# FFN weights compared in the opening, and the first tile's first FFN layer computed among the last tile's steps

## The reference

```python
xz = einsum('bld,ed->ble', x, in_proj_w)           # 256 -> 2 x 512, x and z
xc = silu(depthwise_conv4(x) + conv_b)             # u
dt_lo, B, C = split(einsum(u, x_proj_w), 64, 16, 16)
delta = softplus(einsum(dt_lo, dt_proj_w) + dt_proj_b)
h_t = exp(delta_t * A) * h_{t-1} + (delta_t * u_t) * B_t;  y_t = h_t . C_t   # 512 x 16 states
x1 = layernorm(x + einsum((y + u * D) * silu(z), out_proj_w))
h = silu((x1 @ w1) * s1) * ((x1 @ w2) * s2)        # 256 -> 1024
h = gelu((h @ h1) * sh1);  h = gelu((h @ h2) * sh2)   # 1024 -> 1024, twice
out = layernorm(x1 + (h @ w3) * s3)                # 1024 -> 256
```

## Time and profile before

| | us |
|---|---|
| median of 3 runs | 3138.71 (3132.48 to 3142.14) |
| profiled execution | 3133.98, span 3131.2 |
| PE, DVE, ACT, POOL busy | 2717.2, 2348.0, 2005.7, 1757.6 |
| first scan starts | 78.65 |
| last scan ends | 1963 |
| first matmul of the second stage | 2042.71 |

### The profile page before, as it was taken

The page is one execution under the profiler, slowest core; times in us unless marked ns, Lnnn a source line. Parts: engine busy times, 40 slices in busy tenths (PEclk is TensorE's granted clock), DMA queues, the critical chain, the costliest instruction groups (busy, mean ns, idle before and its releaser), DMA issues. The chain is left out here.

```text
span 3131.2 us, 39976 instructions
## 1 busy us (share of the span) xinstructions
PE 2717.2 (87%) x10900; PEld 1618.7 (52%) x10900; DVE 2348.0 (75%) x2845; ACT 2005.7 (64%) x3326; POOL 1757.6 (56%) x902
## 2 busy tenths in 40 slices
PE   5787887888887888888888885599999999999997
PEld 2243343333343343343333332478888888888886
DVE  2999999999999999999999999535444444444442
ACT  3767777767777767777777776545555545556542
POOL 0899899999899899899999899300000000000000
PEclk8788988988988889889889887799999999999999
DMA  5365466565465466465475465632222222222210
GB/s 136 92 189 160 121 190 160 126 182 150 121 193 162 124 180 162 115 194 150 130 191 144 133 188 166 247 107 81 86 75 67 94 67 80 88 72 74 87 41 14
DMA packets 236287, 402.54 MB, mean 129 GB/s; under 512 B 22977, under 2 KB 62145, under 8 KB 236097
## 3 DMA queue, kind: packets, MB, share of 16 engines
q1 hardware_dynamic: 174336, 293.48, 34.8%
q10 hardware_dynamic: 61760, 106.98, 10.6%
HBM read 276.12 MB, written 124.26 MB: 128 GB/s over the span
## 5 line engine op out<-in xcount | busy, mean ns | idle before, releaser
L1181 DVE TENSOR_TENSOR_SCAN h<-bank,state,db 128x512 f32<-128x512 f32 x1024 | 1252.9, 1266 | 61.5 <-ACT bank L863 34.4
L1044 POOL TENSOR_TENSOR hc<-h,c_rows 128x1024 f32<-128x1024 f32 x512 | 1200.7, 2375 | 28.1 <-PE bank L634 18.0
L863 ACT ACTIVATE bank<-d_bc,a_neg 128x512 f32<-128x512 f32 x1024 | 691.4, 685 | 345.8 <-DVE h L1181 230.5
L1523 ACT ACTIVATE s_h<-s_bank,sc 128x512 f32<-128x512 f32 x256 | 175.9, 687 | 494.0 <-PE s_bank L1462 493.7
L1462 PE MATMUL s_bank<-s_mid,h_r 128*128 128x512 f32 x2048 | 467.0, 389 | 0.0
L703 PE MATMUL bank<-x_t,w 128*128 128x512 f32 x1024 | 386.0, 506 | 75.1 <-ACT ab L933 35.9
L1165 DVE TENSOR_TENSOR db<-bank,du_bc 128x2048 f32<-128x2048 f32 x192 | 435.0, 2266 | 15.5 <-DMA du_bc<-du_rows 15.5
L1462 PEld LDWEIGHTS s_bank<-s_mid,h_r 128*128 128x128 f32 x2048 | 384.4, 188 | 80.1
L1055 POOL TENSOR_TENSOR db<-du_bc,b_row 128x2048 f32<-128x2048 f32 x64 | 291.0, 4547 | 104.3 <-DVE h L1181 98.6
L634 PE MATMUL bank<-hc,fold_w 128*32 128x512 f32 x2048 | 334.5, 732 | 7.2 <-DVE u L1205 4.4
L613 PE MATMUL bank<-bc,w_spread 64*128 64x512 f32 x272 | 154.4, 575 | 210.2 <-DVE db L1165 205.9
(11 more groups left out here) (140 smaller groups left out, 3584.1 us busy)
## 6 DMA issues: line engine op xcount, KB each, us to landing
ab<-ab ACTq DMA_DIRECT2D x264, 256.0 KB, 4.2
du_bc<-du_rows SPq DMA_DIRECT2D x256, 256.0 KB, 4.9
d_bc<-d_rows SPq DMA_DIRECT2D x256, 256.0 KB, 8.1
s_abr<-ab SPq DMA_DIRECT2D x120, 512.0 KB, 3.8
w<-w ACTq DMA_DIRECT2D x128, 256.0 KB, 3.6
d_rows<-sp_r SPq DMA_DIRECT2D x64, 256.0 KB, 2.0
du_rows<-sp_w SPq DMA_DIRECT2D x64, 256.0 KB, 2.0
x<-res SPq DMA_DIRECT2D x17, 512.0 KB, 9.3
```

The source lines that it names most:

```text
L863: act.activation(decays[DECAY_BANK[g]][:], d_bc[c % 2][:, j, :], ACT.Exp, scale=a_neg[:, g:g + 1]).then_inc(decay, 1)
L1044: pool.tensor_tensor(hc[:, k % HCSTEPS, at:at + HG], h[:, H_SLOT[k], at:at + HG], c_rows[:, q, :].unsqueeze(1).broadcast_to([P, HG, NT]), ...
L1181: dve.tensor_tensor_scan(h[:, H_SLOT[k], j, :], decays[DECAY_BANK[g]][:], db[:, k % DBSTEPS, j, :], state[:, g:g + 1], ALU.mult, ALU.add). ...
L1523: act.activation(hring[c % RING][:], p_h[m % HBANKS][:], ACT.Gelu, scale=sc[:, 2 + layer, m:m + 1]).then_inc(gelu, 1)
```

## The change

- Opening: SP loads all 18 pieces of h1, h2 and w3 behind w1 and w2 (`open_raw`, in the places of d_bc, du_bc, db, h, hc), POOL casts each into one of two buffers (`open_piece`), DVE compares (`check`): 14 pieces and the pieces of w1 before BEFORE's slots, four at slot 28. SP's first `copies` wait for 8 comparisons. The second rounding of w1/w2 pieces by ACT moves from slot 8 to 30, its comparison to slot 32.
- Last tile: ACT rounds h1's eight pieces at slots 8, 12, ..., 36; SP loads the first three ahead of `copies(t, 3)`, ACT's own queue the other five, a slot after a rounding. `first_abr` lies elsewhere. At slot 51 TensorE computes the first output of the first tile's h1 layer. ACT loads the table of Ln and Exp at slot 48.
- After it, the seven other outputs of that layer stand among norm, transposes and gate products (`closing` of pe and act); their gelu and high part on ACT, their low part on DVE behind the flag. h2's and w3's ten pieces are loaded by SP through three places instead of four and rounded by POOL, not compared; then the gate weights 2 to 7 are loaded in the places of the raw pieces (they were all eight loaded before). PAST's products use 4 banks instead of 8 and the copies a ring of 3 instead of 7. The end of these stores is waited for by SP in the second stage.
- Second stage: the first tile begins with `hidden(first, 1)`; the second tile's gate is made within that layer (`gate_steps`). First and second tile are unrolled, the loop begins at the third.

```diff
-W12_SLOTS = (2, 8)
+W12_SLOTS = (2, 30)
+CHECKS_FIRST, CHECK_SLOT, CHECK_W2_SLOT = 14, 28, 32
+ROUND_SLOTS = (8, 12, 16, 20, 24, 28, 32, 36)
+RAW_PLACES = 3
+GATE_SLOT, FIRST_SLOT = 42, 51
+FIRST_BANKS = (5, 6, 7, 3)
-PAST_RING = 7
-PAST_BANKS = (0, 3, 4, 5, 6, 7, 2, 1)
+PAST_BANKS = (0, 4, 2, 1)
 # sync, opening
+            for j in range(PIECES):
+                if open_bytes[j] == sb.first_byte["db"]:
+                    sp.wait_ge(consts, 1)
+                load_piece(sp, open_raw[j][:], j).then_inc(open_in[j], 16)
+            sp.wait_ge(checked, 8)
             copies(OPENING, 0)
 # sync, last tile and after
+                if t is LAST_ROW[-1]:
+                    closing_loads(t)
                 copies(t, 3)
...
             def closing(t):
                 for m in range(KH):
+                    if m == 2:
+                        sp.wait_ge(decay, t.count(NG, 3 * GC + DECAY0))
...
+                    elif m == 6:
+                        sp.wait_ge(h1_round, H1_PIECES)
                     sp.dma_start(first_abr[m][:], ...)
+                sp.wait_ge(first_lo, KH)
+                for j in range(RAW_PLACES + EARLY_POOL_PIECES):
+                    load_pool(j)
+                store_x1(PAST)
+                for j in range(RAW_PLACES + EARLY_POOL_PIECES, H2_PIECES + W3_PIECES):
+                    load_pool(j)
+                sp.wait_ge(pool_round, H2_PIECES + W3_PIECES)
+                for m in range(2, KH):
+                    sp.dma_start(past_w12[m][:].bitcast(F32), w12[m]).then_inc(past_w12_in, 16)
 # tensor
+            def first_layer(m):
+                if m >= len(FIRST_BANKS):
+                    pe.wait_ge(mid_gelu, m - len(FIRST_BANKS) + 1)
+                for k in range(KH):
+                    if m == 0:
+                        pe.wait_ge(first_lo, k + 1)
+                    for j in range(2):
+                        last = pe.matmul(bank[FIRST_BANKS[m % len(FIRST_BANKS)]][:], ...)
+                last.then_inc(mid_mm, 1)
+
+            def closing():
+                for m in (1, 2, 3):
+                    first_layer(m)
+                for k in range(KM):
+                    transposed(PAST, k, 0)
...
+                pe.matmul(p_y[:, 0:2 * KM + PIECES], ones[:], losses[:], start=True, stop=True).then_inc(counted, 1)
+                first_layer(4)
+                for k in range(KM):
+                    transposed(PAST, k, 2)
+                first_layer(5)
+                for e in range(AB):
+                    if e in (4, 8):
+                        first_layer(5 + e // 4)
+                    ffn_product(PAST, e)
 # scalar
+            def first_layer(m):
+                act.wait_ge(mid_mm, m + 1)
+                if m >= len(hring):
+                    act.wait_ge(mid_lo, m - len(hring) + 1)
+                act.activation(hring[m % len(hring)][:], ..., ACT.Gelu, ...).then_inc(mid_gelu, 1)
+                act.wait_ge(mid_gelu, m + 1)
+                act.activation(mid[0][:, m, :], hring[m % len(hring)][:], ACT.Copy).then_inc(mid_hi, 1)
+
+            def closing():
...
+                first_layer(5)
+                for e in range(AB):
+                    if e in (4, 8):
+                        first_layer(5 + e // 4)
+                    copy_product(PAST, e)
+                    store(PAST, e)
 # gpsimd
+            def open_piece(j):
+                pool.wait_ge(open_in[j], 16)
+                if j >= 2:
+                    pool.wait_ge(checked, j - 1)
+                pool.tensor_copy(open_r[j % 2][:], open_raw[j][:]).then_inc(open_round, 1)
+
+            for j in range(CHECKS_FIRST + 2):
+                open_piece(j)
             tile(BEFORE)
 # second stage
+        if t is not first:
+            return [(layer, m - 1)] if m else []
+        return [[], [(0, 0)], [(0, 1), (0, 2)], [(0, 3), (0, 4)], [(1, 0)], [(1, 1), (1, 2)], [(1, 3), (1, 4)], []][m]
...
+        for store_done, count in kept.stores:
+            sp.wait_ge(store_done, count)
...
+            pe.sem_inc(h_mm, KH)
+            hidden(first, 1)
+            output(first)
+            tile(second)
```

More of the change, by code:

```diff
@@ L366, in product_before @@
                     return before
+        kept.stores += [(ab_out[k], PAST.count(ab_uses(k), ab_uses(k) + ABOUT0)) for k in range(ABRING)]
         block = ctx.enter_context(nc.Block())
@@ L748, in _ @@
                 tile(t)
[L749 to L757, removed]
+            closing()
         @block.scalar
@@ L1100, in tile @@
                     n = OFF + i
+                    if t is BEFORE and i == CHECK_SLOT:
+                        for j in range(CHECKS_FIRST + 2, PIECES):
+                            open_piece(j)
                     if n % JC == 0:
@@ L1274, in tile @@
                         norm(t, i)
+                    if t is BEFORE and i == CHECK_SLOT:
+                        for j in range(CHECKS_FIRST, PIECES):
+                            check(j)
+                    if t is BEFORE and i == CHECK_W2_SLOT:
+                        for piece in range(KM, 2 * KM):
+                            check_w12(piece)
                     now, g = at_group(t, n)
@@ L1295, in tile @@
                         closing(t, i)
-            for piece in range(2 * KM):
-                check_w12(piece)
+            for j in range(CHECKS_FIRST):
+                if j == CHECKS_FIRST // 2:
+                    for piece in range(KM):
+                        check_w12(piece)
+                check(j)
             tile(BEFORE)
@@ L1379, in split_stage @@
     first = PairTile(0, 0)
+    second = first.following()
     last_pair = [PairTile(STEPS - 1, tt) for tt in range(2)]
@@ L1436, in body @@
             load(first)
-            load_half(first.following(), 0)
-            with sp.Fori(0, STEPS - 1) as b:
+            load_half(second, 0)
+            tile(first)
+            tile(second)
+            with sp.Fori(1, STEPS - 1) as b:
                 for tt in range(2):
@@ L1526, in hidden @@
                     act.activation(dst[:, m, :], hring[c % RING][:], ACT.Copy).then_inc(hi, 1)
-                    if m and exists(t.following()):
+                    if exists(t.following()):
                         if layer == 0 and m == 1:
                             act.wait_ge(o_mm, t.count(SUB, OUT0))
-                        gated(t.following(), layer, m - 1)
-            with act.Fori(0, STEPS - 1) as b:
+                        for half, step in gate_steps(t, layer, m):
+                            gated(t.following(), half, step)
+            hidden(first, 1)
+            hidden(second, 0)
+            hidden(second, 1)
+            with act.Fori(1, STEPS - 1) as b:
                 for tt in range(2):
@@ L1622, in tile @@
                 norm(t)
-            with dve.Fori(0, STEPS - 1) as b:
+            hidden(first, 1)
+            residual(first)
+            norm(first)
+            tile(second)
+            with dve.Fori(1, STEPS - 1) as b:
                 for tt in range(2):
```

253 lines of the change are left out of this document (130 added, 123 removed).

## The result

The median of six runs is 3120.1 us (3118.9 to 3124.2), against 3140.4 us (3132.5 to 3145.4) for the kernel before on the same chip: a ratio of 0.994, with a 95% interval of 0.9924 to 0.9957. That is 20.3 us less where 23.1 were predicted, and 3120.1 where 3115.6 was. The profiled execution took 3118.93 us, its span 3114.7, 16.5 less than before.

A forecast was written before the change was run, and what follows sets the result against it. Scans on DVE and POOL set the pace to 1966 us, TensorE from 2042.7, with a seam between. Terms -30.9 + 2.9 + 1.5 + 2.4 + 1.0 = -23.1 took the median 3138.71 to 3115.6 us; range 3103 to 3128.

The forecast's parts named there:

- The seam: Between last tile and second stage: with the first layer moved in, the second layer starts at 2043.9, not 2074.75; -30.9 us.
- the ring of three: Rival, chance 0.04: seam product copies wait for stores landing after 9.2 us; +8.8 us, 3147.5.
- The clock: At the stage border: TensorE idles 5.5 us, its clock falls and the first block runs slower; +2.9 us.
- The last tile: ACT's added roundings and load issues mostly covered, h1 loads meeting group 3's copies; +1.0 us, ends 0 and 5.2.
- the h1 loads of slots 17 to 25 meet the du_bc and d_bc copies of group 3: Last tile step: of one or two loads of 1.3 us beside these copies, 0.9 us are covered.
- the 4 us that I had named as a sign of being wrong: Sign: a last tile longer by over 4 us would show the prediction wrong.
- The gate: Second tile's gate made within one layer of the second stage instead of two; +1.5 us, ends 0 and 3.9.
- gate late: Rival, chance 0.12: loads land in 6.2 us and ACT loses another 5.5 us in that layer; -15.2 us, 3123.5.
- the last lands 3.8 us later at T+26.8: Gate step: second half's loads, issued T+19.6 to T+23 after the stage's start T, all land by T+26.8.
- the 1 to 4 us that I had said would show it: Sign: output of the first tile comes 1 to 4 us late behind ACT.
- The opening: Before the first scan: casts and checks take turns, and checks delay POOL's two multiplications; +2.4 us, ends 0 and 21.8.
- each microsecond there is one of the first scan: Opening step: POOL's two multiplications each wait for one check, and the first scan comes 2.4 us later.

The follow-up runs named there:

- experiment four: Changed kernel with the first tile's first FFN layer put back in the second stage, weight comparisons still in the opening; 3130.3 us, kernel before 3129.4 beside it.
- Experiment eight: Changed kernel with the seam's sixteen product stores issued by SP instead of ACT, with seven places instead of three; single run 3112.9 us.
- experiment six: Changed kernel with the second tile's products loaded directly, its eight silus in one block, and 14 useless matmuls before the stage border; 3103.4 us.
- experiment three: Changed kernel with eight useless matmuls on TensorE behind the last gate product, before the stage border; single run 3122.4 us.

## Why the prediction was right, and where its terms were not

**The seam** (-30.9 forecast, -31.7 measured) went in the order written: the out-projection's second half 1 us later than the last tile's own shift, the norm without table loads in front of it, copies 1.07 us apart, no wait for a store, the border at 2048.26, which less the 5.2 us that the earlier stages were late is 2043.1 against 2043.9. Two small errors met in it. ACT's last copy ended at 2045.75, by the same shift 1.5 us earlier than written, mostly because TensorE was 1.1 us quicker up to group 7; and from there to the first matmul it took 2.5 us where I had 1.82. By experiment four, 8 us of the 31.7 are the comparisons' and the rest is the layer's.

I had put the start of harm from the ring of three at a landing of 2.2 us, and the point where it undoes the whole gain at 7.6. The sixteen stores of the changed kernel landed in 2.0 us (median). In three of nine traces a single store came late and cost about 2 us, so the rival's mechanism is real at a small size. Experiment eight takes it away.

**The clock** (+2.9 forecast, +2.8 measured). TensorE was idle for 4.5 us and the layer began at 0.5 (1.2 GHz). The 5.5 us of idle time in the prediction do not follow from its own numbers: 2032.3 and eight products of 0.91 us give 2039.6, 4.3 us before its border. A shorter gap, which I tried later, did not save it: with 1.9 us the layer still took 30.7 us (experiment six). Why the clock fell in each case is not shown beyond these rows.

**The last tile** (+1.0 forecast, +4.8 measured) is the first mis-sized term. The step that failed is "the h1 loads of slots 17 to 25 meet the du_bc and d_bc copies of group 3 ... 0.9 us of the one or two loads of 1.3 us are covered". I counted the load's own bytes. The harm was in front of the copies: the du_rows store landed 2.6 us later beside a 512 KB load, everything behind it on SP's queue was issued later by that, and d_bc then met two more loads (1928.06 and 1932.52) and landed in 10.1 us instead of 7.9. In all eight traces with a load 0.2 us ahead of the store, du_bc was issued 4.6 to 4.8 us behind it, in the four others 2.0. The ends of the range (up to 5.2) held the term, but it is beyond the 4 us that I had named as a sign of being wrong.

**The gate** (+1.5 forecast, +6.7 measured) is the second, and the rival "gate late" is what happened, by its first half. The step that failed is "the last lands 3.8 us later at T+26.8". With T the stage's start, the last of the second half landed at T+29.8:

```profile
s_abr<-ab SPq DMA_DIRECT2D x4, 512.0 KB, 5.2
...
2071.53 6.54 DMA s_abr<-ab
...
2078.09 0.72 ACT L1618 ACTIVATE s_abr<-s_abr,sc 128x512 f32<-128x512 f32 x1 [0.53 <-DMA s_abr<-ab]
...
2085.39 0.58 PE L1580 MATMUL s_bank<-w_r,first_hi 128*128 128x256 f32 x1 [2.62 <-DVE first_lo L1693]
...
2070.96 1.28 ACT L1618 ACT_TABLE_LOAD   x1
2072.25 0.72 ACT L1618 ACTIVATE s_abr<-s_abr,sc 128x512 f32<-128x512 f32 x1
```

First the median from issue to landing, then the piece of the chain that is a transfer, then ACT's last wait for one, then TensorE's for a low part, and at the end a table load with the silu behind it. The four loads are issued within 3 us on one queue, and the last takes 6.5 us, near the 6.2 of the earlier trace rows and not 3.8. With 6.5 in its place my sum gives 4.2 us, not 6.7. ACT's gelus 5 to 7 were 3 us late by that. TensorE then waited three times, 0.9, 2.6 and 1.0 us, where I had taken only the last low part as what counts, so the output came later than the 1 to 4 us that I had said would show it; the other 2.2 us go with matmuls at a lower clock between and behind these waits (0.50 from 2085 to 2090 us). The other half of the rival did not come: with four table loads in the layer and direct transfers, the time behind it was 9.2 us, 0.8 above that of before. It was an estimate of 5.5 us, from the drain of 1.38 us that the Trainium skill ("ScalarE: Activation LUTs", What ACT_TABLE_LOAD costs) adds to every switch; the trace does not agree, since ACT's copy ends at 2070.95, the load starts at 2070.96, and the next silu starts at 2072.25, 1.29 us behind it.

**The opening** (+2.4 forecast, +0.5 measured; in the ten other traces the first scan came at 78.8 to 80.9, so 0.2 to 2.2). Casts and checks took turns:

```profile
27.16 2.03 DVE L1318 SCALAR_TENSOR_TENSOR open_raw<-open_raw,open_r 128x1024 f32<-128x1024 f32 x1 [0.93 <-POOL open_r L1212]
...
29.11 1.21 DVE L1318 SCALAR_TENSOR_TENSOR open_raw<-open_raw,open_r 128x1024 f32<-128x1024 f32 x1
...
58.09 2.18 POOL L1139 TENSOR_TENSOR sp_r<-sp_r,sp_e 128x512 f32<-128x512 f32 x1 [5.05 <-DVE sp_e L1280]
```

Two pairs take 4.10 us (27.16 to 31.26 for the next), so 2.05 a pair against my 2.26, and DVE was free at 51.9, not 54.9. The Trainium skill ("SBUF — State Buffer", SBUF: two separate sides) says that a DVE operation with two SBUF inputs and a GpSimd one that reads SBUF exclude each other for a whole instruction. The trace agrees: a check that starts beside a cast takes 2.03 us, the next one 1.21. POOL's two multiplications took 0.9 us longer each, where I had 1.2; with 0.7 us that the first step size was late and 0.7 of a slower store, du_bc was issued 3.2 us later. The step that failed is that each microsecond there is one of the first scan; the transfers behind made up most of it (du_bc landed in 5.9 us instead of 7.7, d_bc in 8.8 instead of 10.5).

**The whole.** By stage dates the change is worth 17 us and not 23. The medians differ by 20 because the profiled execution of before, from which the sum was made, lay 6.4 us below the median of its runs in that comparison and that of after only 1.2 below. The predicted time was 4.5 us too low for a sum 6.1 us too good.

## What to carry to other kernels

A load that nobody waits for can still cost several microseconds (4.8 here): look at which store, on any queue, is about to land when it is issued, and who is queued behind that store. Where a ring of buffers carries loads whose place comes free late, take the landing time of the last of the burst (here 6.5 us) and not that of one (3.8), and ask what every waiting group on TensorE costs, not only the last. Where an untouched loop varies by more than the terms do, compare dates between marks of a stage.

## What the runs showed of the hardware

The 256 KB store of du_rows was followed by the copy that waits for it after 2.0 us in four traces, and after 4.6 to 4.8 us in the eight with a 512 KB load issued 0.2 us earlier on another queue. The granted clock stayed at 1.0 through a gap of 4.7 us and then fell to 0.55 while TensorE was at work again (experiment three), and after a gap of 1.9 us it fell too (0.68 and 0.63 in the next two stretches of 2.5 us, experiment six), so a slow stretch can begin only when the engine is at work again. Fifteen equal tiles of the loop took between 1768 and 1783 us in twelve profiled executions.
